# Second attention: a ring of four single banks for the row scores

## The reference

```
q, k, v = (x @ W)                      # split into 16 heads of 16
scores = q @ k^T ; scores[causal] = -inf
attn   = softmax(scores / sqrt(16)) ; ctx = attn @ v ; out = ctx @ W_out + b_out
```

## Time and profile before

| | |
|---|---|
| median of 3 runs | 1340.27 us (1336.17 to 1340.35) |
| the profiled execution | 1338.22 us |
| its span | 1336.5 us |
| granted TensorE clock, mean | 0.976 of full speed |
| PE, DVE, ACT, POOL busy | 93%, 61%, 44%, 37% of the span |
| the 256 maxima (L1584) | 184.4 us busy, 52.8 idle before them |
| the stage of the change | lead-in from 767, tiles from 805 to 1058 us |

### The profile page before, as it was taken

How to read it: one execution, slowest core, us unless ns; L and a number is a source line. 1 busy time by engine, 2 the same in 40 slices (tenths; PEclk the granted TensorE clock), 3 DMA queues, 4 the chain that set the end, 5 groups by cost and what they waited for, 6 DMA issues and landing times. The chain is left out here.

```text
span 1336.5 us, 18196 instructions
## 1 busy us (share of the span) xinstructions
PE 1237.3 (93%) x5912; PEld 853.8 (64%) x5912; DVE 814.8 (61%) x1718; ACT 588.3 (44%) x1089; POOL 491.6 (37%) x351
## 2 busy tenths in 40 slices
PE   6999999999999999999998988899898878999887
PEld 5866888888888788888886622233222246778665
DVE  6577764444444344444446686877778586976465
ACT  2322443333333333333333525677667653443553
POOL 3101355555555455555554330111111143454000
PEclk9999989999999999999999987999999999999899
DMA  4010243334433533333440441222220210110001
GB/s 155 23 39 1 80 126 111 110 110 110 110 110 82 127 110 111 108 111 110 109 110 1 142 142 57 65 64 66 65 64 18 72 59 25 48 46 14 1 16 48
DMA packets 49420, 102.73 MB, mean 77 GB/s; under 512 B 8516, under 2 KB 21700, under 8 KB 49356
## 3 DMA queue, kind: packets, MB, share of 16 engines
q1 hardware_dynamic: 49228, 101.81, 27.1%
q10 hardware_dynamic: 128, 0.13, 0.0%
HBM read 88.59 MB, written 8.93 MB: 73 GB/s over the span
## 5 line engine op out<-in xcount | busy, mean ns | idle before, releaser
L479 DVE TENSOR_TENSOR q_t<-q_t,ps 128x512 f32<-128x512 f32 x132 | 90.7, 687 | 228.9 <-ACT q_t L420 226.5
L1584 DVE CUSTOM_DVE_ANT_0 masked<-ps,causal 128x128 f32<-128x128 f32 (+7 forms) x256 | 184.4, 756 | 52.8 <-PE ps L1405 52.0
L537 POOL TENSOR_TENSOR wqkv<-q_t,v_tok 128x512 f32<-128x512 f32 x132 | 200.0, 1529 | 29.4 <-DVE q_t L479 18.6
L527 POOL TENSOR_TENSOR d_w_lo<-raw,d_w_hi 128x768 fp32r<-128x768 f32 x66 | 122.5, 1855 | 239.6 <-ACT d_w_hi L391 239.6
L471 DVE TENSOR_TENSOR wqkv_lo<-wqkv,wqkv_hi 128x512 fp32r<-128x512 f32 x132 | 156.0, 1182 | 67.5 <-ACT wqkv_hi L397 67.5
L313 PE MATMUL ps<-h_hi,d_w_hi 128*128 128x512 f32 x528 | 166.4, 395 | 3.0 <-POOL d_w_lo L527 1.1
L313 PE MATMUL ps<-h_lo,d_w_hi 128*128 128x512 f32 x528 | 165.6, 394 | 0.0
L313 PE MATMUL ps<-h_hi,d_w_lo 128*128 128x512 f32 x528 | 165.6, 394 | 0.0
L1564 ACT ACTIVATE xn<-ps 128x512 f32<-128x512 f32 (+3 forms) x256 | 117.3, 512 | 58.1 <-PE ps L1425 56.3
L391 ACT CAST d_w_hi<-raw 128x768 fp32r<-128x768 f32 x66 | 55.0, 833 | 194.6 <-PE ps L326 192.9
L313 PEld LDWEIGHTS ps<-h_hi,d_w_hi 128*128 128x128 f32 x528 | 98.7, 188 | 27.0 <-POOL d_w_lo L527 3.1
(11 more groups left out here) (257 smaller groups left out, 2131.0 us busy)
## 6 DMA issues: line engine op xcount, KB each, us to landing
v_tok<-router_weights_t SPq DMA_DIRECT2D x132, 256.0 KB, 3.9
raw<-in_moe SPq DMA_DIRECT2D x66, 384.0 KB, 4.2
qk<-qk_parts SPq DMA_DIRECT2D x72, 128.0 KB, 2.7
qk_parts<-parts SPq DMA_DIRECT2D x16, 384.0 KB, 2.7
raw<-in_mlp SPq DMA_DIRECT2D x16, 384.0 KB, 3.1
h_t<-qk_parts SPq DMA_DIRECT2D x24, 128.0 KB, 2.6
x_tok<-in_x SPq DMA_DIRECT2D x4, 512.0 KB, 8.2
out_x<-x_tok SPq DMA_DIRECT2D x8, 256.0 KB, 2.2
```

The source lines that it names most:

```text
L479: nc.vector.tensor_tensor(prod[:, s % 3, :], sg[:, s % 3, :], ps[:, 2 * (s % 2) + 1, :], ALU.mult).then_inc(s_t, 1)
L527: nc.gpsimd.tensor_tensor(w_lo[:, slot, :], raw[:, slot, :], w_hi[:, slot, :].bitcast(F32), ALU.subtract).then_inc(s_wlo, 1)
L537: nc.gpsimd.tensor_tensor(inter[:, s % 3, :], prod[:, s % 3, :], wbc[:, s // 2, (s % 2) * GW:(s % 2 + 1) * GW], ALU.mult).then_inc(s_int, 1)
L1584: nc.vector.tensor_tensor_reduce(masked[:, at % 2, 0:k], ps[:, bank:bank + 2, :].rearrange("p a n -> p (a n)")[:, 0:k], causal[:, SEQ - k: ...
```

## The change

The four banks 0, 1, 6 and 7 become a ring of single positions (`S_RING`). A narrow entry (blocks 0 to 3, and the row block) takes the next position; a wide one takes the next aligned pair (positions 0 and 1 or 2 and 3), skipping a position where needed. At build time a table says for each entry its first position (`s_at`) and the latest entry that used any of the banks it takes (`s_free`), and PE waits for that one. DVE's instruction reads one bank of a narrow block and two of a wide one; the columns that it reads are the same as before.

```diff
-                s_bank = [0, 6]
+                S_RING = (0, 1, 6, 7)
+                s_at, s_used, s_free = [], [None] * 4, []
+                for n, (v, i) in enumerate(entries):
+                    wide = i < HQ * TB and i % TB >= 4
+                    first = (s_at[-1] + (2 if s_wide else 1)) % 4 if s_at else 0
+                    first = (first + 1) % 4 // 2 * 2 if wide else first
+                    s_at.append(first)
+                    s_wide = wide
+                    taken = range(first, first + (2 if wide else 1))
+                    s_free.append(max((s_used[p] for p in taken if s_used[p] is not None), default=None))
+                    for p in taken:
+                        s_used[p] = n
+                row_bank = lambda at: S_RING[s_at[at]]
...
-                            bank = s_bank[at % 2]
+                            bank = row_bank(at)
...
-                            if at >= 2:
-                                pe.wait_ge(s_mx, at - 1)
+                            if s_free[at] is not None:
+                                pe.wait_ge(s_mx, s_free[at] + 1)
...
-                            bank = s_bank[at % 2]
+                            bank = row_bank(at)
...
-                                masked[:, at % 2, 0:k], ps[:, bank:bank + 2, :].rearrange("p a n -> p (a n)")[:, 0:k],
+                                masked[:, at % 2, 0:k], ps[:, bank:bank + (k + GW - 1) // GW, :]
+                                .rearrange("p a n -> p (a n)")[:, 0:k],
```

## The result

The changed kernel takes 1322.21 us (median of 4 runs, 1321.03 to 1327.64) against 1339.3 before; the ratio is 0.9884, 95% interval 0.9856 to 0.9911. In a second series it was 0.9894 (0.9877 to 0.9912). The medians of the first series lie 17.1 us apart; by the ratios the gain is 15.5 and 14.2 us, and the intervals reach from 11.9 to 19.3 and from 11.8 to 16.5. Forecast were 1326 and 13.1. Lines have moved by 12 or 13: L1417 is the row-score matmul, L1407 the row block's transposition, L1437 the transposed scores, L1596 the maximum, L1589 the row block's copy.

What follows compares the result with a forecast made beforehand. PE's in-order queue, stalled by row-score blocks waiting for DVE's maxima, was taken as the bound. Rounds and lead-in: 7.6 + 1.8 + 1.8 + 0.95 + 0.95 = 13.1 us, forecast 1326, own range 1321 to 1330, overall 1321 to 1333.

Steps and rivals of the forecast that it cites:

- (a): Round 933 to 964, block B3 at 939.00: needs only B7, long done, so its wait goes; gain 0.40 us.
- (b): Same round, B1 at 945.36: goes at once, while B2 now needs B7; gain 0.42, say 0.40 us.
- (c): Same round, third head: B1 and B3 lose about 0.1 us of wait each; taken as 0.15, between 0 and 0.25.
- (d): B1 of the next group's first head, at 959.86: needs only B6; gain 0.95 us.
- B1 at 844.77: Round from 840: B1 waits 1.22 us, but B2 close behind needs the same B7, so only about 0.3 comes back.
- lead-in: 767 to 802, DVE alone works through 32 blocks: third block gains 0.3, last head's B1 and B3 0.65; together 0.95 us.
- price of 0.24 us for each us at the low level: Slowdown in the rounds at the low clock level (1.2 GHz), taken from the first two rounds: 0.24 us a us.
- nothing gives the gain back: After 1023 no row-score block is left; later work follows in the same order and moves as a whole.
- B7 gates it anyway: Rival: B2 and B3 still need B7, so a round gains about 0.95 us, about 6.5 in all: 1333; chance 0.15.
- ACT is the real wait: Rival: each released wait ends on the three banks of the transposed scores instead; 1339, no change; chance 0.08.
- The clock: Rival: the new pattern of waits loses full clock in the rounds; slower, 1348 (three rounds) or 1362; chance 0.05.
- DVE's idle before B4 and B0's wait stay: In the rounds: B0's wait for B6 stays; DVE's idle before B4 mostly stays, coming from PE's order, not the bank.

Runs made afterwards that it cites:

- ring with the old waits: Changed kernel's ring banks and one-bank reads kept, but every block waits again for the maximum two places back: 1338.35 us, ratio 1.000 to the kernel before.
- B1 alone: Changed kernel with only B1 (the 256-column block) keeping its released wait, all others waiting two places back: 1331.34 us, ratio 0.9951 to the kernel before.
- weighted places: Changed kernel with blocks handed out over the tiles by cost, not evenly: 1330.56 us, ratio 0.9942 to the kernel before; with finer steps 1332.09, 0.996.

## Why the prediction was right, point by point

**The waits, step by step.** That the table only loosens waits, and that banks cost nothing by themselves, was right (ring with the old waits: 1.000). The four cases of a round were right in place and nearly in size: (a) 0.40 against 0.42, (b) 0.40 against 0.42, (c) 0.15 against 0.21, (d) 0.95 against 1.01. In (b) B1 goes at once and B2 stays behind B7, as foretold. Timeline of PE, kernel after, answering to the earlier trace rows:

```profile
932.69 0.27 PE L1417 MATMUL ps<-h_t 96*128 96x256 bf16 x1
...
933.04 0.34 PE L1417 MATMUL ps<-h_t 96*128 96x384 bf16 x1
```

That B2 waited shows in its weight load, from the timeline of PEld, kernel after:

```profile
933.03 0.10 PEld L1417 LDWEIGHTS ps<-h_t 96*128 96x128 bf16 x1 [0.24 <-DVE hmax L1596]
```

One small step failed, in the second round. There the prediction gave B1 at 844.77 about 0.3 back, and nothing came back. In the kernel after B1 goes at once and B2 has the wait. The next head's B0 starts 10.59 us behind the copy at 833.89, where before it started 10.60 behind that at 840.02. Timeline of PE, kernel before, then after:

```profile
850.62 0.23 PE L1405 MATMUL ps<-h_t 96*128 96x128 bf16 x1 [0.43 <-DVE hmax L1584]
```

```profile
838.84 0.34 PE L1417 MATMUL ps<-h_t 96*128 96x384 bf16 x1 [1.04 <-DVE hmax L1596]
...
844.48 0.23 PE L1417 MATMUL ps<-h_t 96*128 96x128 bf16 x1 [0.43 <-DVE hmax L1596]
```

**The sum.** Four rounds 7.6 against 8.24; first 1.8 against 1.94; second 1.8 against 1.66; last 0.95 against 1.05; lead-in 0.95 against 1.14. Together 13.1 against 14.0. The cases of a round are the term that was sized too small, by 0.16 a round; they made up for the 0.3 that did not come back in the second round. That the first round's 1.8 was met so closely is in part luck. With the old waits in the rounds it took 37.76 to 39.35 us in four profiles, with the released ones 34.45 to 35.87 in three, and within each group the longer ones are those with more time at the low clock. An estimate that takes off the prediction's price of 0.24 us for each us at the low level gives 34.1 to 34.4 against 31.9 to 32.3, a gain of about 2.2.

**Against the time.** The profile shows 16.2, which is 2.2 more than 14.0. Of this, 3.1 is what the profile before had lost besides. The first maximum came at 767.84 against 766.46, 1.4 later: 0.5 of it is there by 700 us, ahead of the stage, and the rest goes with a clock of 0.89 against 1.00 at 735 to 750 us, which other profiles of the changed kernel also have. The low stretch at 769 took 1.7 (from the first maximum to the ninth 9.86 us, against 8.18 in the ring with the old waits at full clock); whether the change removes it is the question left open above. Then 0.9 is lost again behind the stage, where the prediction said that nothing gives the gain back. I had set the clock at nothing in the lead-in and only reckoned with it as a loss. By the ratios the gain is 14.2 and 15.5, and 14.0 lies inside both intervals. The time of 1322.21 against the forecast 1326 owes part of its closeness to these unpredicted pieces.

**The rivals.** *B7 gates it anyway*: no, B1 alone is worth 1.19 a round; only the case at 844.77 went that way, and there wholly (second round 1.66 in place of 1.8). *ACT is the real wait*: no, 2.0 us more of ACT cost 0.06. *The clock*: the rounds stayed at 1.00. The Trainium skill's rule on cycling through PSUM banks ("TensorE: Matmul & The Clock Gate", "A second HAM failure mode: psum-queue depth-cycling") does not show in the rounds here (granted clock 1.00 from 840 to 1010 us in the kernels before and after), and the "no further gain" from PSUM double-buffering ("HAM oscillation — how this bites in real kernels") is not what this kernel shows: ratio 0.9884.

**A claim too strong.** I said that DVE's idle before B4 and B0's wait stay because of PE's order and B6. In the changed kernel both did: B0's wait is 4.8 us as before, and DVE's idle before B4 is 14.8 us of 17.9. But "stay" was too strong as a rule. With the blocks of a head in another order both shrank (0.2 us of idle before B0, 8.6 before B4), and the round became only 0.14 shorter. The expectations that followed made the opposite mistake and took what was left of the waits for time that could be had; the weighted places made the round 1.1 longer.

## What to carry to other kernels

When an in-order queue feeds a consumer through a ring, list for each slot which earlier item frees it, and look for the small items that wait behind a big one: letting a narrow block take one bank instead of a pair let PE go on past the 1.23 us maximum of the widest block. Work one round through row by row with what would be late next, and multiply; do not add up the drawn idle, which leaves out about 0.16 us for each wait that goes. Check where a released wait lands: behind B1 it sometimes came back whole at B2. And waits that are left in a profile are not yet time to be gained: here another order moved them and the round stayed within 0.14 us.

## What was not expected of the hardware

The clock's low stretch that follows the lead-in varies in length between executions whatever the waits: over 790 to 826 us the mean granted clock was 0.57 to 0.76 in the fourteen profiles, and the first round took 39.35 us in one profile with the old waits and 37.76 in another. That difference of 1.6 us is more than the lead-in's whole gain of 0.9 to 1.1, which may be why the times could not show it.
